# Group norm of each image moved from VectorE to ScalarE and GpSimd in the loop over chunks of a two-layer state-space model

## The chip, the cores and the metric

The kernel runs on one core of one Trainium2 chip. Time is device time in microseconds (us), as the median of several executions. The engines of the core are TensorE (PE in the profile), VectorE (DVE), ScalarE (ACT), GpSimd (POOL) and SyncE (SP), which issues most DMAs. Each engine has its own stream of instructions, worked off in order; they wait for each other by semaphores.

## The reference, cut to what matters

An image tensor x of shape (4, 128, 64, 64), called (b, t, n, f), goes through four residual layers. Layers 0 and 1 are the ones that the change is about: a group norm over (t, n) and pairs of features, then a Mamba block along t for each of the 4 x 64 sequences.

```python
def _gn(v, G=32, eps=1e-5):          # v: (B, H, W, C)
    g = v.reshape(B_, H_, W_, G, C_ // G)
    m = jnp.mean(g, axis=(1, 2, 4), keepdims=True)
    s = jnp.var(g, axis=(1, 2, 4), keepdims=True)
    return ((g - m) / jnp.sqrt(s + eps)).reshape(v.shape)

x = x + _L0_conv_ref(_gn(x), ...)    # Mamba, 64 features in, 128 inner, 16 states
x = x + _L1_conv_ref(_gn(x), ...)    # the same with other weights
x = x + _L2_conv_ref(_gn(x), ...)    # top 25 pixels of 16 blocks, two large products
x = x + _L3_conv_ref(_gn(x))         # attention at three scales
```

Mamba is h = exp(dt * A) * h + dt * u * B, y = sum over states of h * C, for 16 states of each of 128 channels.

## The kernel before, in words

X stays in SBUF all the time: 128 partitions are t, and one image is 4096 columns (n, f). Layers 0 and 1 are one loop, `mamba_layers`: an image is cut into 8 chunks of 8 sequences, which makes 32 chunks for each layer and 64 in all (`TOTAL`). A chunk is worked in 16 units, one for each state: a decay on ScalarE (line 742), a drive on VectorE (772) or, for the five states of `POOL_UNITS`, on GpSimd (820), a scan on VectorE (786), the product with C on GpSimd (826), and the sum on TensorE (660). Beside unit s of chunk c stands step s of the preparation of chunk c + 1 (`*_prep`: u, B and C, dt, z), and the gate (791) and the addition to X (795) of chunk c - 1. Every engine's order within a unit is written out in `act_both`, `dve_unit`, `pool_unit` and `pe_unit`. Four buffers of state and of decay let the engines run a few units apart.

The norm is a class, `ImageNorm`. Job j belongs to image j mod 4; jobs 0 to 3 are the input of layer 0, 4 to 7 that of layer 1, and 8 and 9 already images 0 and 1 of layer 2. A job is 32 `bn_stats` on VectorE (206), short VectorE steps on 128 x 32 numbers (217 to 242) with two sums over partitions on TensorE and a Ln and Exp on ScalarE between, and the turning of scale and bias into one column for each feature (251, 265, 276). `NORM_AT` says in which chunk a job begins; its steps are spread over four chunks by `STEP_AT`, and all 32 `bn_stats` stand together at the end of unit 15 of every eighth chunk (and of chunks 0 and 4). Job 0 is done in `prepare`, a block of its own in front of the loop, beside the turning of the weights; the block ends for all engines together. There SyncE issues the load of all four images at once, and ScalarE the 18 small loads of weights.

Layer 2 begins with a group norm on VectorE again (`GroupNorm`, lines 93 to 135, called in `top_blocks`); before, it does images 2 and 3 only (`first` = 2). TensorE's part of it stands behind the scores and fourteen turned pairs.

## Time and profile before

| | us |
|---|---|
| median of 3 executions | 6269.2 (6269.18 to 6271.9) |
| the profiled execution, its own time | 6272.24 |
| span of the profile | 6270.4 |
| first drive of chunk 0 (line 772) starts | 85.09 |
| first drive of chunk 63, the last, starts | 3817.41 |
| granted TensorE clock, mean | 0.932 |

The profile is of one execution. Its times count from the start of the span. "Busy" is the time in which an engine executes something; "idle before" is the engine's gap in front of an instruction, with what released it. The loop over chunks takes 3.73 ms of the 6.27 ms; layer 2 and layer 3 (attention) follow. A chunk is best measured from its first drive to that of the next.

### The profile page before, as it was taken

To read this page: it belongs to the slowest core of one execution; us is meant where nothing else is said; L and a number is where in the kernel's file an instruction comes from. 1 tells how busy PE (TensorE), PEld (TensorE's weight loads), DVE (VectorE), ACT (ScalarE), POOL (GpSimd) and SP (SyncE) were. 2 spreads that over 40 slices of the span, in tenths; PEclk is the share of its full clock that TensorE was granted. 3 is DMA by queue.
4 is the path that set the end of the run, shared out by engine and by line. 5 is a ranking of instruction groups with operands and counts; after the bars stand their busy time and mean duration, and the time that the engine had idled before them with its cause. 6 is when DMAs were issued, how large, how long until landed. Compare 5 with 4: busy or idle time off the path is not lost. (4 is left out here: it accounts for less than half of the span.)

```text
span 6270.4 us, 72602 instructions
## 1 busy us (share of the span) xinstructions
PE 5117.5 (82%) x22494; PEld 2648.8 (42%) x22494; DVE 5045.7 (80%) x7034; ACT 3286.3 (52%) x3657; POOL 4771.9 (76%) x2169
## 2 busy tenths in 40 slices
...
GB/s 154 190 188 184 183 192 205 190 185 205 190 187 205 186 188 205 189 188 206 186 193 206 195 193 155 124 404 74 72 93 164 189 166 190 181 173 189 189 188 209
DMA packets 1424093, 1152.34 MB, mean 184 GB/s; under 512 B 1216728, under 2 KB 1226096, under 8 KB 1415792
## 3 DMA queue, kind: packets, MB, share of 16 engines
...
q8 instruction: 105, 1.72, 0.1%
...
HBM read 814.23 MB, written 21.09 MB: 133 GB/s over the span
## 5 line engine op out<-in xcount | busy, mean ns | idle before, releaser
L826 POOL TENSOR_TENSOR mamba_state<-mamba_state,mamba_c_row 128x1024 f32<-128x1024 f32 x1024 | 2408.9, 2364 | 221.4 <-DVE mamba_state L786 212.0
L660 PE MATMUL mamba_y_ps<-mamba_state,ident 128*128 128x512 f32 x4096 | 2003.9, 616 | 28.5 <-POOL mamba_state L826 28.2
L1721 POOL TENSOR_TENSOR l3s_el<-l3s_s_sb,l3s_eh 128x1024 f16<-128x1024 f32 (+2 forms) x584 | 1169.5, 2013 | 1119.3 <-ACT l3s_s_sb L1706 1113.2
L786 DVE TENSOR_TENSOR_SCAN mamba_state<-mamba_decay,mamba_b_ps 128x1024 f32<-128x1024 f32 x704 | 1607.7, 2284 | 64.3 <-DVE mamba_b_ps L772 2.4
L660 PEld LDWEIGHTS mamba_y_ps<-mamba_state,ident 128*128 128x128 f32 x4096 | 789.5, 196 | 853.4 <-issue 689.2
L1729 DVE TENSOR_SCALAR_CACHE_REDUCE l3s_s_sb<-l3s_s_ps 128x512 f32<-128x512 f32 (+1 forms) x1096 | 753.2, 688 | 479.4 <-PE l3s_s_ps L1665 455.0
L1678 PE MATMUL l3s_o_ps<-l3s_vt,l3s_et 128*128 128x257 f16 x4368 | 879.7, 279 | 189.9 <-DMA l3s_et<-l3s_el 124.8
L742 ACT ACTIVATE mamba_decay<-mamba_dt,mamba_A 128x1016 f32<-128x1016 f32 x704 | 785.9, 1133 | 292.3 <-POOL mamba_dt L807 190.7
L1705 ACT ACTIVATE l3s_eh<-l3s_s_sb,l3s_shift 128x1024 f16<-128x1024 f32 (+2 forms) x584 | 634.6, 1087 | 535.8 <-DMA l3s_et<-l3s_el 423.7
L648 PE MATMUL mamba_b_ps<-mamba_bc,mamba_pick 128*128 128x512 f32 x1408 | 580.7, 495 | 400.2 <-DVE mamba_state L786 392.8
L772 DVE TENSOR_TENSOR mamba_b_ps<-mamba_dtu,mamba_b_ps 128x1024 f32<-128x1024 f32 x704 | 850.4, 1208 | 32.8 <-PE mamba_b_ps L648 31.7
L1680 PE MATMUL l3s_o_ps<-l3s_vt,l3s_et 128*128 128x129 f16 x4368 | 788.5, 224 | 0.0
L820 POOL TENSOR_TENSOR mamba_b_row<-mamba_b_row,mamba_dtu 128x1024 f32<-128x1024 f32 x320 | 755.2, 2360 | 0.1
L786 DVE TENSOR_TENSOR_SCAN mamba_state<-mamba_b_ps,mamba_b_row 128x1024 f32<-128x1024 f32 x320 | 729.3, 2279 | 3.5 <-POOL mamba_b_row L820 1.6
L1706 ACT ACTIVATE l3s_s_sb<-l3s_s_sb,l3s_shift 128x1024 f32<-128x1024 f32 (+2 forms) x584 | 630.0, 1079 | 0.0
L1678 PEld LDWEIGHTS l3s_o_ps<-l3s_vt,l3s_et 128*128 128x128 f16 x4368 | 434.9, 100 | 438.2 <-issue 214.9
L648 PEld LDWEIGHTS mamba_b_ps<-mamba_bc,mamba_pick 128*128 128x128 f32 x1408 | 234.3, 200 | 863.0 <-DVE mamba_state L786 567.6
L1663 PE MATMUL l3s_s_ps<-l3s_xh 128*128 128x512 f16 (+1 forms) x1096 | 428.0, 390 | 94.3 <-DVE l3s_xl L1642 71.4
L1680 PEld LDWEIGHTS l3s_o_ps<-l3s_vt,l3s_et 128*128 128x128 f16 x4368 | 435.2, 100 | 109.9 <-issue 5.7
L1664 PE MATMUL l3s_s_ps<-l3s_xl,l3s_xh 128*128 128x512 f16 (+1 forms) x1096 | 427.2, 390 | 0.0
L1665 PE MATMUL l3s_s_ps<-l3s_xh,l3s_xl 128*128 128x512 f16 (+1 forms) x1096 | 426.2, 389 | 0.0
L742 ACT ACTIVATE mamba_b_ps<-mamba_dt,mamba_A 128x1016 f32<-128x1016 f32 x320 | 351.5, 1098 | 0.0
...
## 6 DMA issues: line engine op xcount, KB each, us to landing
mamba_c_row<-mamba_c_rows SPq DMA_DIRECT2D x1024, 512.0 KB, 3.7
mamba_b_row<-mamba_c_rows SPq DMA_DIRECT2D x320, 512.0 KB, 4.8
...
l_ring_a<-in_L_conv_W SPq DMA_DIRECT2D x14, 704.0 KB, 12.7
l2b_ring_b<-in_L_conv_W SPq DMA_DIRECT2D x13, 704.0 KB, 12.7
...
```

The source lines that it names most:

```text
L648: last = nc.tensor.matmul(b_ps[s % PAIRS][:, half(h)], C["pick"][:, DVE_UNITS.index(s) * P:(DVE_UNITS.index(s) + 1) * P], bc[:, par, half( ...
L660: last = nc.tensor.matmul(y_ps[:, half(h)], C["ident"][:, :], state[:, s % STATES, half(h)], start=False, stop=(s == S - 1))
L742: nc.scalar.activation(seq(to), seq(dt[:, par, :]), ACT.Exp, scale=weights(c)["A"][:, s:s + 1]).then_inc(s_decay, 1)
L772: nc.vector.tensor_tensor(b_ps[s % PAIRS][:, :], dtu[:, par, :], b_ps[s % PAIRS][:, :], ALU.mult).then_inc(s_drive, 1)
L786: nc.vector.tensor_tensor_scan(state[:, s % STATES, :], by, add, 0.0, ALU.mult, ALU.add).then_inc(s_scan, 1)
L820: nc.gpsimd.tensor_tensor(row, row, dtu[:, par, :], ALU.mult).then_inc(s_bdrive, 1)
L826: nc.gpsimd.tensor_tensor(state[:, s % STATES, :], state[:, s % STATES, :], c_row[:, s % C_ROWS, :], ALU.mult).then_inc(s_hc, 1)
L1678: high = lambda stop: nc.tensor.matmul(o_ps[par][:, 0:2 * P + 1], et[:, 0, slot, j, :], vt[:, mt, 0:2 * P + 1], start=(mt == 0), stop=stop)
L1680: lows = lambda: nc.tensor.matmul(o_ps[par][:, P:2 * P + 1], et[:, 1, slot, j, :], vt[:, mt, P:2 * P + 1], start=False, stop=False)
L1705: nc.scalar.activation(eh[:, part, off:off + EXPW], src, ACT.Exp, bias=shift[:, par:par + 1]).then_inc(s_eh, 1)
L1721: nc.gpsimd.tensor_tensor(el[:, part, off:off + EXPW], s_sb[:, par, j * EXPW:(j + 1) * EXPW], eh[:, part, off:off + EXPW], ALU.subtract).t ...
L1729: nc.vector.tensor_scalar(s_sb[:, par, kb * W:(kb + 1) * W], s_ps[(par * NB + kb) % SLOTS][:, 0:W], 0.0, None, ALU.add, ALU.max, accum_out ...
```

## The change

- In the loop VectorE has nothing of the norm any more. For layer 1 (jobs 4 to 7) the statistics of an image are taken by ScalarE in 64 passes over 128 x 128 numbers: 32 that add up the values of a pair of features, and 32 that add up the squares of the distance from the partition's own mean (`scalar_stats`). They are spread over eight chunks, 8 for each chunk (`stat_at`, `STAT_UNITS`).
- The short steps of a job are ten on ScalarE (`scalar`) and six on GpSimd (`gpsimd`), spread over five chunks by `ACT_AT` and `POOL_AT`.
- The statistics of images 1 to 3 for layer 0 stay `bn_stats` on VectorE, but all stand in the preparation of chunk 0, in front of steps 4, 10 and 13 (`SECOND_STATS`), each with six short steps behind them.
- `ImageNorm` no longer does jobs 8 and 9: the norm in front of layer 2 takes all four images.
- SyncE loads image 0 first, and the other three when all weights have landed.
- In `prepare`, the chain of job 0 goes over ScalarE and GpSimd, and the second layer's weights are turned behind its first two sums.

```diff
+    def vector_stats(self, dve, j):
+
+        nc, mine, m2 = self.nc, self.mine[:, self.groups(j)], self.m2[:, self.groups(j)]
+        for g in range(G):
+            nc.vector.bn_stats(out=self.stats[:, g * 6:(g + 1) * 6],
+                               in_=self.Xv[:, j, :, 2 * g:2 * g + 2]).then_inc(self.s_stats, 1)
+        dve.wait_ge(self.s_stats, G * (j + 1))
+        st = self.stats.rearrange("p (g k) -> p g k", k=6)
+        nc.vector.tensor_tensor(self.dev[:, :], st[:, :, 1], st[:, :, 4], ALU.subtract)
+        nc.vector.tensor_tensor(m2, st[:, :, 2], st[:, :, 5], ALU.add)
+        nc.vector.tensor_tensor(mine, st[:, :, 1], st[:, :, 4], ALU.add).then_inc(self.s_join, 1)
+        dve.wait_ge(self.s_join, 3 * j + 1)
+        nc.vector.tensor_scalar(mine, mine, 0.5, None, ALU.mult)
+        nc.vector.tensor_tensor(self.square[:, :], self.dev[:, :], self.dev[:, :], ALU.mult).then_inc(self.s_join, 1)
+        dve.wait_ge(self.s_join, 3 * j + 2)
+        nc.vector.scalar_tensor_tensor(m2, self.square[:, :], N / 2.0, m2, ALU.mult, ALU.add).then_inc(self.s_join, 1)
+
+    def scalar_stats(self, act, j, k):
+
+        nc, later = self.nc, j - B
+        image = self.Xv[:, j % B, :, :]
+        group = lambda g: image[:, :, 2 * g:2 * g + 2]
+        over = self.over.rearrange("p (n e) -> p n e", e=2)
+        g = k % G
+        if k < G:
+            wait(act, self.s_first, G * later + g)
+            if g == 0:
+                wait(act, self.s_second, G * later)
+            nc.scalar.activation(over, group(g), ACT.Identity, accum_out=self.sums[:, g:g + 1]).then_inc(self.s_first, 1)
+            return
+        if g == 0:
+            act.wait_ge(self.s_first, G * (later + 1))
+            nc.scalar.activation(self.mine[:, self.groups(j)], self.sums[:, :], ACT.Identity,
+                                 scale=0.5 / N).then_inc(self.s_centre, 1)
+            nc.scalar.activation(self.minus[:, :], self.sums[:, :], ACT.Identity, scale=-0.5 / N).then_inc(self.s_centre, 1)
+            act.wait_ge(self.s_centre, 2 * (later + 1))
+        wait(act, self.s_second, G * later + g)
+        at = j % B * G + g
+        nc.scalar.activation(over, group(g), ACT.Square, bias=self.minus[:, g:g + 1],
+                             accum_out=self.m2[:, at:at + 1]).then_inc(self.s_second, 1)
...
+    def scalar(self, act, ps, j, i):
...
+            act.wait_ge(self.s_sum, 3 * j + 1)
+            op = nc.scalar.activation(self.mean[:, :], ps[:, 0:G], ACT.Identity, scale=1.0 / P)
...
+        if i in (7, 8):
+            act.wait_ge(self.s_pool, pool_done + 6)
+            src = (self.scale_g, self.bias_g)[i - 7][0:1, self.groups(j)]
+            for copy in range(2):
+                dst = self.rows[0:1, i - 7, copy * F:(copy + 1) * F].rearrange("p (g e) -> p g e", e=2)
+                op = nc.scalar.activation(dst, src.unsqueeze(2).to_broadcast([1, G, 2]), ACT.Identity,
+                                          scale=(1.0, -1.0)[i - 7])
...
+    def gpsimd(self, pool, j, i):
+        nc, act_done, pool_done = self.nc, ACT_STEPS * j, POOL_STEPS * j
+        square, root, m2 = self.square[:, :], self.root[:, :], self.m2[:, self.groups(j)]
+        scale, bias = self.scale_g[:, self.groups(j)], self.bias_g[:, self.groups(j)]
+        if i == 0:
+            pool.wait_ge(self.s_act, act_done + 1)
+            op = nc.gpsimd.tensor_tensor(self.dev[:, :], self.mine[:, self.groups(j)], self.mean[:, :], ALU.subtract)
+        if i == 1:
+            pool.wait_ge(self.s_act, act_done + 3)
+            if j >= B:
+                pool.wait_ge(self.s_second, G * (j - B + 1))
+            op = nc.gpsimd.tensor_tensor(m2, m2, square, ALU.add)
...
+ACT_STEPS, POOL_STEPS = 10, 6
...
             @block.sync
             def _(sp):
                 for b in range(B):
+                    if b == 1:
+                        for i in range(2):
+                            sp.wait_ge(s_load[i], len(WEIGHTS) * 16)
                     sp.dma_start(X[:, b * PIX:(b + 1) * PIX], ins["x"][b].rearrange("t n f -> t (n f)")).then_inc(s_x[b], 16)
 
             @block.gpsimd
...
+                norm.constants(pool)
+                for i in range(POOL_STEPS):
+                    norm.gpsimd(pool, 0, i)
...
+                act.wait_ge(norm.s_const, 2)
+                for i in range(ACT_STEPS):
+                    norm.scalar(act, sum_ps[(0, 0, 0, 1, 1, 1, 1, 0, 0, 0)[i]], 0, i)
...
+                scale_taps(0)
                 dve.wait_ge(s_x[0], 16)
-                for g in range(G):
-                    norm.stat(0, g)
-                norm.step(dve, 0, 0)
+                norm.vector_stats(dve, 0)
                 copy_turned(0)
-                norm.step(dve, 0, 1)
-                norm.step(dve, 0, 2)
-                norm.read(dve, sum_ps[0], 0, 0)
-                for i in range(3, 6):
-                    norm.step(dve, 0, i)
+                scale_taps(1)
...
+                turn(0)
                 pe.wait_ge(s_one, 1)
                 norm.sum(pe, sum_ps[0], 0, 0)
-                pe.wait_ge(s_wdt[0], 1)
-                nc.tensor.matmul(f_ps[0][:, 0:D], wx[0][0:R, :], wdt_t[0][:, :], start=True, stop=True).then_inc(s_fused[0], 1)
+                fuse(0)
                 norm.sum(pe, sum_ps[1], 0, 1)
-                pe.wait_ge(s_wdt[1], 1)
-                nc.tensor.matmul(f_ps[1][:, 0:D], wx[1][0:R, :], wdt_t[1][:, :], start=True, stop=True).then_inc(s_fused[1], 1)
+                turn(1)
                 norm.sum(pe, sum_ps[0], 0, 2)
+                fuse(1)
...
+NORM_AT = [None] + [5 * (j - 1) for j in range(1, B)] + [PER_IMAGE * (j - B + 2) + 1 for j in range(B, 2 * B)]
+NORM_JOB = {first + phase: (j, phase) for j, first in enumerate(NORM_AT) if first is not None for phase in range(5)}
+SECOND_STATS = {4: 1, 10: 2, 13: 3}
+SUM_AT, SUMS = 14, {0: 0, 1: 1, 3: 2}
+ACT_AT = ({}, {1: 0, 6: 1, 7: 2}, {1: 3, 2: 4, 6: 5, 13: 6}, {6: 7, 7: 8}, {1: 9})
+POOL_AT = ({}, {3: 0, 10: 1}, {8: 2, 10: 3, 15: 4}, {1: 5}, {})
+STAT_UNITS = (2, 6, 7, 10, 13, 14, 15, 16)
+
+
+def stat_at(c, s):
+
+    if s == 0:
+        c, s = c - 1, S
+    if s not in STAT_UNITS or c <= PER_IMAGE:
+        return None
+    j, slot = divmod((c - PER_IMAGE - 1) * len(STAT_UNITS) + STAT_UNITS.index(s), 2 * G)
+    return (j + B, slot) if j < B else None
...
-                    wait(pe, norm.s_read, norm_reads_before(n - 1))
...
+            stat = stat_at(c, s)
+            if stat:
+                if stat[1] == 0:
+                    act.wait_ge(s_add, PER_IMAGE * (stat[0] - B + 1))
+                norm.scalar_stats(act, *stat)
+
+        def pool_norm(pool, c, s):
+            j, phase = NORM_JOB.get(c, (None, None))
+            if j is not None and s in POOL_AT[phase]:
+                norm.gpsimd(pool, j, POOL_AT[phase][s])
 
...
         def act_both(act, c, par, s, prep):
             act_unit(act, c, par, s)
+            act_norm(act, c, s)
             if prep:
                 act_prep(act, c + 1, 1 - par, s)
-            act_norm(act, c, s)
...
-            dve_norm(dve, c, s)
...
-            dve_stats(dve, c, s)
...
+            pool_norm(pool, c, s)
...
                 for k in range(S):
-                    if k == 4:
-                        dve.wait_ge(s_x[1], 16)
-                        for g in range(G):
-                            norm.stat(1, g)
+                    if k in SECOND_STATS:
+                        dve.wait_ge(s_x[SECOND_STATS[k]], 16)
+                        norm.vector_stats(dve, SECOND_STATS[k])
                     dve_prep(dve, 0, 0, k)
...
-                           offset[:, :, :, :].rearrange("p a r k -> p (a r k)")[:, 0:B * G * 6], temps, pick_ps[0], pick_ps[1], 2)
+                           offset[:, :, :, :].rearrange("p a r k -> p (a r k)")[:, 0:B * G * 6], temps, pick_ps[0], pick_ps[1])
```

VectorE before, at the border of chunks 16 and 17, where job 5 begins. `mamba_state` is the scan, `X<-X` the addition of a finished chunk.

```order
L795 TENSOR_TENSOR X<-X,mamba_prep_ps 128x512
L786 SCALAR_TENSOR_TENSOR mamba_state<-mamba_decay,mamba_b_ps 128x1024
L206 BN_STATS mamba_norm_stats<-X 128x6 x32
L772 TENSOR_TENSOR mamba_b_ps<-mamba_dtu,mamba_b_ps 128x1024
L786 SCALAR_TENSOR_TENSOR mamba_state<-mamba_decay,mamba_b_ps 128x1024
L772 TENSOR_TENSOR mamba_b_ps<-mamba_dtu,mamba_b_ps 128x1024
L217 TENSOR_TENSOR mamba_norm_dev<-mamba_norm_stats 128x32
L218 TENSOR_TENSOR mamba_norm_spread<-mamba_norm_stats 128x32
L219 TENSOR_TENSOR mamba_norm_pair_sum<-mamba_norm_stats 128x32
```

The same place in the changed kernel:

```order
L840 TENSOR_TENSOR X<-X,mamba_prep_ps 128x512
L831 SCALAR_TENSOR_TENSOR mamba_state<-mamba_decay,mamba_b_ps 128x1024
L817 TENSOR_TENSOR mamba_b_ps<-mamba_dtu,mamba_b_ps 128x1024
L831 SCALAR_TENSOR_TENSOR mamba_state<-mamba_decay,mamba_b_ps 128x1024
L817 TENSOR_TENSOR mamba_b_ps<-mamba_dtu,mamba_b_ps 128x1024
L831 SCALAR_TENSOR_TENSOR mamba_state<-mamba_decay,mamba_b_ps 128x1024
L836 TENSOR_TENSOR mamba_yz<-mamba_sz,mamba_y_ps 128x1024
```

All the `norm` rows of this place are gone from VectorE, and the scans and drives follow each other.

GpSimd before, from the drive of the last of its states in a chunk (`mamba_b_row` is a drive, `mamba_state` a product, `mamba_ln_e` and `mamba_dt` preparation):

```order
L820 TENSOR_TENSOR mamba_b_row<-mamba_b_row,mamba_dtu 128x1024
L826 TENSOR_TENSOR mamba_state<-mamba_state,mamba_c_row 128x1024 x3
L803 TENSOR_TENSOR mamba_ln_e<-mamba_ln_e,mamba_gu 128x1024
L826 TENSOR_TENSOR mamba_state<-mamba_state,mamba_c_row 128x1024
L807 TENSOR_TENSOR mamba_dt<-mamba_ln_e,mamba_dt 128x1024
L826 TENSOR_TENSOR mamba_state<-mamba_state,mamba_c_row 128x1024
L813 TENSOR_TENSOR mamba_dtu<-mamba_dt,mamba_u 128x1024
```

The same place in the changed kernel, in a chunk with the third phase of a job:

```order
L871 TENSOR_TENSOR mamba_state<-mamba_state,mamba_c_row 128x1024 x2
L865 TENSOR_TENSOR mamba_b_row<-mamba_b_row,mamba_dtu 128x1024
L323 TENSOR_TENSOR mamba_norm_square<-mamba_norm_root 128x32
L871 TENSOR_TENSOR mamba_state<-mamba_state,mamba_c_row 128x1024 x2
L326 TENSOR_TENSOR mamba_norm_square<-mamba_norm_square,mamba_norm_var 128x32
L871 TENSOR_TENSOR mamba_state<-mamba_state,mamba_c_row 128x1024
L848 TENSOR_TENSOR mamba_ln_e<-mamba_ln_e,mamba_gu 128x1024
L871 TENSOR_TENSOR mamba_state<-mamba_state,mamba_c_row 128x1024
L852 TENSOR_TENSOR mamba_dt<-mamba_ln_e,mamba_dt 128x1024
L871 TENSOR_TENSOR mamba_state<-mamba_state,mamba_c_row 128x1024
```

Two of the six short steps of a job stand here between products of 128 x 1024.

ScalarE before, units 6 to 9 of a chunk. `mamba_decay` and `mamba_b_ps` are decays, the rest preparation.

```order
L742 ACTIVATE mamba_b_ps<-mamba_dt,mamba_A 128x8x127
L742 ACTIVATE mamba_decay<-mamba_dt,mamba_A 128x8x127
L738 ACTIVATE mamba_b_ps<-mamba_zero 128x8
L742 ACTIVATE mamba_b_ps<-mamba_dt,mamba_A 128x8x127
L706 ACTIVATE mamba_dt<-mamba_prep_ps,mamba_b_dt 128x1024
L708 ACTIVATE mamba_prep_ps<-mamba_prep_ps,mamba_b_dt 128x1024
L710 ACTIVATE mamba_prep_ps<-mamba_prep_ps 128x1024
L742 ACTIVATE mamba_decay<-mamba_dt,mamba_A 128x8x127
```

The same place in the changed kernel, in one of the chunks 9 to 41; the rows with `norm_sums` are the new passes over X:

```order
L787 ACTIVATE mamba_b_ps<-mamba_dt,mamba_A 128x8x127
L243 ACTIVATE mamba_norm_shared,mamba_norm_sums<-X 128x128
L787 ACTIVATE mamba_decay<-mamba_dt,mamba_A 128x8x127
L243 ACTIVATE mamba_norm_shared,mamba_norm_sums<-X 128x128
L783 ACTIVATE mamba_b_ps<-mamba_zero 128x8
L787 ACTIVATE mamba_b_ps<-mamba_dt,mamba_A 128x8x127
L751 ACTIVATE mamba_dt<-mamba_prep_ps,mamba_b_dt 128x1024
L753 ACTIVATE mamba_prep_ps<-mamba_prep_ps,mamba_b_dt 128x1024
L755 ACTIVATE mamba_prep_ps<-mamba_prep_ps 128x1024
L787 ACTIVATE mamba_decay<-mamba_dt,mamba_A 128x8x127
```

The two passes of units 6 and 7 stand behind the decays of these units, in front of the step that waits for dt.

## Rows read from the trace of the kernel before

**Rows 1.** Rows of the page, part 1: busy us (share of the span) xinstructions.

```profile
PE 5117.5 (82%) x22494; PEld 2648.8 (42%) x22494; DVE 5045.7 (80%) x7034; ACT 3286.3 (52%) x3657; POOL 4771.9 (76%) x2169
```

**Rows 2.** Busy time by window: bounds, length; PE, PEld, DVE, ACT, POOL busy (x); clock, DMA.

```profile
824.89:1052.57 227.68, 198.55 (x558) 89.65 (x556) 219.43 (x133) 126.23 (x140) 223.07 (x96) 0.97 0.58 201
...
3185.08:3469.59 284.51, 246.93 (x695) 112.00 (x693) 274.15 (x166) 158.43 (x176) 278.93 (x120) 0.97 0.58 201
...
3648.09:3817.41 169.32, 146.81 (x414) 66.22 (x412) 164.37 (x100) 94.65 (x105) 167.28 (x72) 0.98 0.57 200
...
85.09:3817.41 3732.32, 3148.02 (x8733) 1421.46 (x8731) 3618.36 (x2531) 1990.70 (x2224) 3515.71 (x1511) 0.96 0.56 192
```

**Rows 3.** Groups by line, 0 to 4200 us: busy, mean ns | idle before, releaser.

```profile
L826 POOL TENSOR_TENSOR mamba_state<-mamba_state,mamba_c_row 128x1024 f32<-128x1024 f32 x1024 | 2408.9, 2364 | 221.4 <-DVE mamba_state L786 212.0
...
L786 DVE TENSOR_TENSOR_SCAN mamba_state<-mamba_decay,mamba_b_ps 128x1024 f32<-128x1024 f32 x704 | 1607.7, 2284 | 64.3 <-DVE mamba_b_ps L772 2.4
```

**Rows 4.** VectorE in order of time: start, us, line, operation [idle before].

```profile
1003.69 1.20 DVE L791 TENSOR_TENSOR mamba_yz<-mamba_sz,mamba_y_ps 128x1024 f32<-128x1024 f32 x1
...
1030.29 1.20 DVE L760 SCALAR_TENSOR_TENSOR mamba_gu<-mamba_gu,mamba_prep_ps 128x1024 f32<-128x1024 f32 x1
...
1059.67 1.20 DVE L791 TENSOR_TENSOR mamba_yz<-mamba_sz,mamba_y_ps 128x1024 f32<-128x1024 f32 x1
...
1108.68 6.25 DVE L206 BATCH_NORM_STATS2 mamba_norm_stats<-X 128x6 f32<-128x128 f32 x32
```

**Rows 5.** Groups by line, 0 to 4200 us: the norm on VectorE.

```profile
L206 DVE BATCH_NORM_STATS2 mamba_norm_stats<-X 128x6 f32<-128x128 f32 x320 | 62.6, 278 | 0.3 <-PEq L319 0.3
...
L242 DVE SCALAR_TENSOR_TENSOR bias_g<-mamba_norm_mean,scale_g 128x32 f32<-128x32 f32 x10 | 15.1, 1508 | 0.0
...
L240 DVE TENSOR_TENSOR scale_g<-mamba_norm_root,mamba_norm_square 128x32 f32<-128x32 f32 x10 | 13.1, 1308 | 0.0
```

**Rows 6.** GpSimd groups by form: one operation at two sizes.

```profile
L1721 POOL TENSOR_TENSOR l3s_el<-l3s_s_sb,l3s_eh 128x1024 f16<-128x1024 f32 x512 | 1090.2, 2141 | 509.0 <-ACT l3s_s_sb L1706 502.9
...
L1721 POOL TENSOR_TENSOR l3s_el<-l3s_s_sb,l3s_eh 128x256 f16<-128x256 f32 x8 | 5.4, 670 | 477.7 <-ACT l3s_s_sb L1706 477.7
```

**Rows 7.** ScalarE in order of time, the same chunk as group 4.

```profile
1021.14 0.18 ACT L738 ACTIVATE mamba_b_ps<-mamba_zero 128x8 f32<-128x8 f32 x1 [1.93 <-DVE mamba_state L786]
...
1027.51 1.02 ACT L715 ACTIVATE mamba_gu<-mamba_prep_ps 128x1024 f32<-128x1024 f32 x1
```

**Rows 8.** DMA throughput, 0 to 100 us in 40 slices of 2.5 us.

```profile
GB/s 85 344 426 427 426 428 433 434 377 76 4 0 0 3 0 0 0 0 105 0 105 0 0 0 0 0 20 72 265 315 397 243 0 0 7 0 36 346 88 162
```

**Rows 9.** All engines in order of time, the first 46 us.

```profile
6.21 12.96 ACTq L346 DMA_DIRECT2D start_cw<-in_L_conv_conv_w  x1
...
24.80 1.28 ACT L354 ACT_TABLE_LOAD   x1 [24.80 <-issue]
...
28.50 6.26 DVE L206 BATCH_NORM_STATS2 mamba_norm_stats<-X 128x6 f32<-128x128 f32 x32
...
40.50 0.23 ACT L282 ACTIVATE mamba_norm_root<-mamba_norm_var 128x32 f32<-128x32 f32 x1 [13.04 <-DVE mamba_norm_var L274]
...
44.91 0.16 DVE L276 COPY mamba_norm_c<-start_sum_ps 128x2 f32<-128x2 f32 x1 [1.16 <-PE start_sum_ps L265]
```

**Rows 10.** All engines in order of time, preparation of chunk 0.

```profile
76.44 1.22 DVE L760 SCALAR_TENSOR_TENSOR mamba_gu<-mamba_gu,mamba_prep_ps 128x1024 f32<-128x1024 f32 x1 [8.69 <-ACT mamba_gu L715]
...
77.82 2.35 POOL L803 TENSOR_TENSOR mamba_ln_e<-mamba_ln_e,mamba_gu 128x1024 f32<-128x1024 f32 x1 [32.22 <-DVE mamba_gu L760]
...
83.10 1.23 DVE L764 TENSOR_TENSOR mamba_sz<-mamba_prep_ps,mamba_gz 128x1024 f32<-128x1024 f32 x1 [5.44 <-ACT mamba_gz L724]
...
85.09 1.23 DVE L772 TENSOR_TENSOR mamba_b_ps<-mamba_dtu,mamba_b_ps 128x1024 f32<-128x1024 f32 x1 [0.76 <-POOL mamba_dtu L813]
```

**Rows 11.** VectorE in order of time, head of layer 2.

```profile
3887.13 13.09 DVE L102 BATCH_NORM_STATS2 l2a_offset<-X  x64 [4.89 <-PEq L70]
...
3931.13 0.22 DVE L119 SCALAR_TENSOR_TENSOR l2a_shared<-l2a_shared,l2a_pick_ps 128x64 f32<-128x64 f32 x1 [29.72 <-PE l2a_pick_ps L139]
```

More of the change, by code:

```diff
@@ L195, in __init__ @@
+        self.s_second = sem("norm_second_pass")
         self.s_sum = sem("norm_sum_over_partitions")
[L196 to L207 removed]
@@ L209, in step @@
[L209 to L219 removed]
+        self.s_act = sem("norm_scalar_step")
@@ new lines, in sum @@
+    def sum(self, pe, ps, j, k):
+        nc = self.nc
+        if k < 2:
+            if k == 1:
+                pe.wait_ge(self.s_pool, POOL_STEPS * j + 2)
+            elif j < B:
+                pe.wait_ge(self.s_join, 3 * j + 3)
+            else:
+                pe.wait_ge(self.s_centre, 2 * (j - B + 1))
+            src = (self.mine, self.m2)[k]
+            last = nc.tensor.matmul(ps[:, 0:G], self.C["one"][:, :], src[:, self.groups(j)], start=True, stop=True)
+        if k == 2:
+            pe.wait_ge(self.s_act, ACT_STEPS * j + 9)
+            for i in range(2):
+                last = nc.tensor.matmul(ps[:, i:i + 1], self.rows[0:1, i, :], self.C["one"][0:1, 0:1], start=True, stop=True)
+        last.then_inc(self.s_sum, 1)
@@ L254, in sum @@
-    def sum(self, pe, ps, j, k):
-        wait(pe, self.s_read, self.reads(j) + k)
-        if k == 0:
-            pe.wait_ge(self.s_step, NORM_STEPS * j + 1)
-            last = self.nc.tensor.matmul(ps[:, 0:G], self.C["one"][:, :], self.pair_sum[:, :], start=True, stop=True)
-        if k == 1:
-            pe.wait_ge(self.s_step, NORM_STEPS * j + 6)
-            last = self.nc.tensor.matmul(ps[:, 0:G], self.C["one"][:, :], self.spread[:, :], start=True, stop=True)
-        if k == 2:
-            pe.wait_ge(self.s_rows, 8 * (j + 1))
-            for i in range(2):
-                last = self.nc.tensor.matmul(ps[:, i:i + 1], self.rows[0:1, i, :, :].rearrange("p c f -> p (c f)"),
-                                             self.C["one"][0:1, 0:1], start=True, stop=True)
-        last.then_inc(self.s_sum, 1)
@@ L411, in _ @@
                     nc.vector.tensor_copy(C["pick"][:, i * P:(i + 1) * P], pick[:, unit * P:(unit + 1) * P])
-                for i in range(6, NORM_STEPS):
-                    norm.step(dve, 0, i)
-                norm.row(dve, 0, 0)
-                norm.row(dve, 0, 1)
-                norm.read(dve, sum_ps[0], 0, 2)
             @block.tensor
```

177 lines of the change are left out of this document (62 added, 115 removed).

## The prediction

> **What bounds the kernel now.** I read the counts of the page first, then busy time by window, then VectorE, GpSimd and ScalarE in order of time. The page [rows 1] gives VectorE 80% and GpSimd 76% of the span, an average over stages that says little. The windows tell it [rows 2]: each is cut at the first drive of a chunk. Three of them, of 4, 5 and 3 chunks, hold nothing of the norm: 227.68 + 284.51 + 169.32 = 681.5 us for 12 chunks, 56.8 us each, with GpSimd busy 669.3 us (98%) and VectorE 658.0 us (97%). The whole loop up to the last chunk takes 3732.32 us for 63 chunks, 59.2 us each. There VectorE is busy 57.4 us for each chunk, and GpSimd 55.8 us, which is no more than in the windows without a norm. So two engines are almost equally full: GpSimd with 24 operations of 128 x 1024 for each chunk, VectorE with scans and drives [rows 3]. A job of the norm lies on VectorE and stops both: GpSimd's idle time in the loop is nearly all a wait for a scan [rows 3].
>
> The best chunk takes 55.98 us, from gate to gate [rows 4]: the 288 GpSimd operations of the three windows are busy 669.3 us, 2.32 each, and 24 of them are 55.8 us. The 0.8 us that an average chunk without a norm takes above that comes in chunks in which TensorE's clock was granted at the lower level for a while; the windows stand at 0.97 and 0.98 of full speed [rows 2]. I keep these stalls in the forecast.
>
> **The loop.** Removed from VectorE are the 32 `bn_stats` of jobs 2 to 9, 6.25 us at a stretch [rows 4], and some 22 short steps of jobs 1 to 9. The short steps are dear: two of them take 1.5 and 1.3 us for 32 columns [rows 5], while a `bn_stats` over 128 columns takes 0.28. By VectorE's busy time the norm is 57.4 - 54.8 = 2.6 us for each chunk, 164 us in 63. Not all of it comes back, since behind VectorE stands GpSimd at 98%. What comes back is the difference of the periods: 63 x 56.8 = 3578.4, so 3732.3 - 3578.4 = **153.9 us less**.
>
> **GpSimd's new steps.** Jobs 1 to 7 have six each, 42 operations on 128 x 32, on an engine that has no room. The trace has the same operation at 1024 and at 256 columns, 2.141 and 0.670 us [rows 6]: 1.9 ns for each column and 0.18 us fixed, an estimate of 0.25 us at 32. From below stands the fixed part, 0.18 us, from above the 0.67 us of 256 columns: 7.6 to 28 us in all. I take 42 x 0.25 = **10.5 us more**. Their waits: each waits for a ScalarE or GpSimd step placed two or more units earlier, and behind a waiting one stand GpSimd's products, for which TensorE and, over the four state buffers, the scans wait. ScalarE runs ahead of GpSimd, so I put these waits at nothing; if a step waited 1 us each time, it would cost 42 us.
>
> The operations of VectorE in rows 5 with two operands in SBUF take five times as long as the `bn_stats`, which has one. The Trainium skill (SBUF — State Buffer, Who interferes with whom) says that a VectorE instruction with two SBUF inputs and a GpSimd instruction that reads SBUF exclude each other, and that the second one blocks fully; the trace agrees. By that rule GpSimd's new steps too could be held by VectorE, but after the change each VectorE instruction of the loop has at most one operand in SBUF, beside one in PSUM, so the sum would stay as it is; by equal sharing the steps would cost up to the upper bound.
>
> **ScalarE's new work.** 256 passes over 128 x 128, eight for each chunk from 9 to 41, and seven times ten short steps. ScalarE is busy 126.2 us in four chunks [rows 2], 31.6 us of 56.9. A pass with the reading of its sum I put at 0.5 us, above the 0.23 us of 128 x 32 [rows 9] and well under the 1.02 us of 128 x 1024 [rows 7]: 4 us for each chunk, up to 8 us by the upper bound. They cost nothing as long as no decay and no preparation step gets late. The tight place is units 6 and 7: two passes and, in a job, two short steps, 1.5 us, stand in front of a wait of 1.93 us [rows 7]; and behind it the step at line 715 ends at 1028.5 while VectorE takes its result at 1030.29 [rows 4], without a gap in front, 1.8 us later. So 3.7 us of cover against 1.5 us; at the upper bound 2.5 us, still covered. The passes at 13 to 16 stand where ScalarE is ahead of the scans.
>
> **The start.** SyncE's four loads keep the DMA engines at about 430 GB/s until 22.5 us [rows 8], ScalarE's queue is held for 12.96 us at its 11th load, and its table load comes at 24.80 us [rows 9]. With image 0 alone the transfer is over after about 7.5 us (the first three slices of rows 8 hold its 2.1 MB). The held load is then free at about 8.5 us, seven more at 0.6 us each, as the first ten took without a jam (6.21 us), end at 12.7 us, table and first Exp at 14.2 us, and the `bn_stats` of job 0 start at 14.4 instead of 28.50 us [rows 9]: 14.1 us earlier. From there to the last step of the block it was 16.6 us (45.07 - 28.50) [rows 9]. Now: `bn_stats` and joining 7.2 us, the chain over ScalarE, GpSimd and TensorE with some twenty steps of 0.25 to 0.35 us (a short ScalarE step is 0.23 [rows 9]) about 6.5 us, then the last fused product and the copies on VectorE behind it 3 us: 16.7. **14 us less**; between 8 us (a longer chain, ring still jammed) and 17 us.
>
> In chunk 0's preparation VectorE idles 8.69 us before line 760 and 5.44 us before line 764 [rows 10]. The second image's statistics there (6.3 + 1.1 us) fit into the first gap; the third's (7.4 us and more, since GpSimd works beside it from 77.82 us [rows 10]) overrun the second by 2.6 us, with 0.76 us of slack behind it: **2.6 us more**, at most 6. The images have landed by then: issued at 14.5 us, at 430 GB/s until about 30 us.
>
> **Layer 2.** `GroupNorm` takes four images instead of two: 13.09 us more of `bn_stats`. VectorE waits 29.72 us for TensorE right behind it [rows 11], so that is hidden; 64 more columns in ten short steps and a reciprocal behind the wait are **1.2 us more**. At most 3.
>
> **Sum.** -153.9 + 10.5 - 14 + 2.6 + 1.2 = -153.6. The profiled execution's own time is 6272.24 us, 3.0 above the median of the three runs: 6272.2 - 153.6 = 6118.6, and 6115.6 as a median. I predict **6116 us**, a ratio of 0.9755.
>
> **Rivals.** (1) The stalls of the low TensorE clock go with the norm, and the loop settles at 55.98 us a chunk: 63 x 0.82 = 52 us less, 6064. For it: single chunks reach that [rows 4]. Against: the windows without a norm have the stalls too, and average 56.8 [rows 2]. (2) GpSimd is now the only bound, and its steps cost the upper bound and wait: 28 + 21 (0.5 us each), in place of 10.5: 6155. (3) The start gives only 4 us of its 14, because ScalarE's 18 issues or the longer chain over three engines set its end: 6126. (4) The other side: ScalarE's passes are slow, since they read pairs 256 bytes apart, and hold up the preparation. It decides once two passes and two steps at units 6 and 7 exceed 3.7 us; to undo the whole gain, each of 33 chunks must lose 4.6 us, so a pass must take about 4 us. The same reading on VectorE runs at full pace (0.28 us, rows 5). Half of that would leave 6190; all of it 6280. (5) The first `tensor_tensor` on GpSimd now comes in the chain of job 0. In the trace it starts 0.16 us after its release, with 32 us of idle time before it [rows 10]; what may load in that time needs cover, of which about 14 us are left. If none covered it, it would be some 6 us, 6122. The Trainium skill (GPSIMD Engine Reference, Instruction dispatch) says that the first call of newly loaded code costs about 6 us that no row shows; by that rule 6122, if it counts from the call; the trace does not bear that out.
>
> **Chances.** Forecast 58% (own range 6095 to 6140), rival 1 12%, rival 2 14%, rival 3 7%, rival 5 4%, rival 4 5%, of which 2.5% slower than before. Eight in ten lie in 6072 to 6165: all of the forecast and of rivals 3 and 5, most of rival 2, and the nearer part of 1. 0.2% (13 us) is about what a measurement of this kernel can tell from none: faster by more 0.965, within 0.01, slower 0.025.
>
> **What would show it.** Chunks of 56 to 58 us from first drive to first drive, with GpSimd over 97% busy and VectorE at 96%; GpSimd's small steps at 0.2 to 0.3 us and without waits; ScalarE's passes under 0.6 us, and no new wait of VectorE at lines 760 and 764 of the old numbering; `bn_stats` of job 0 at about 14.4 us and the first drive of chunk 0 at about 74 us; the head of layer 2 within 2 us of before. It is wrong if VectorE or GpSimd shows gaps behind ScalarE, if chunks take over 57.5 us, or if the start moves by less than 8 us.

## The result and the profile after

The changed kernel takes 6103.5 us (median of four runs, 6098.0 to 6112.2); the kernel before, beside it on the same chip, 6269.7. The ratio is 0.9736, with a 95% interval of [0.9719, 0.9752]. The prediction said 6116 us and 0.9755. The profiled execution is the slowest of the four, 6112.24 us, where the prediction's sum gave 6118.6: 160.0 us were gained in place of 153.6. The medians lie further apart, 12 us, because the profiled execution is 8.7 us above its median here, and 3.0 us before.

The page, part 1, and busy time by window from the first drive of chunk 0 to that of the last chunk, and for three chunks that follow one another (columns as in [rows 2]):

```profile
PE 5081.1 (83%) x22486; PEld 2628.5 (43%) x22486; DVE 4908.9 (80%) x6708; ACT 3384.9 (55%) x4253; POOL 4779.0 (78%) x2219
```

```profile
73.72:3656.23 3582.51, 3115.66 (x8726) 1404.66 (x8726) 3453.06 (x2079) 2087.51 (x2809) 3518.44 (x1552) 0.97 0.57 201
...
1664.64:1720.62 55.98, 48.44 (x138) 21.84 (x138) 54.73 (x35) 34.56 (x56) 55.93 (x26) 0.98 0.56 204
1720.62:1778.76 58.14, 50.60 (x144) 23.23 (x142) 54.94 (x34) 35.75 (x54) 55.93 (x25) 0.96 0.58 199
1778.76:1835.30 56.54, 49.49 (x138) 22.29 (x138) 54.83 (x35) 34.19 (x51) 55.79 (x24) 0.97 0.57 201
```

Against [rows 2] the loop went from 3732.32 to 3582.51 us, 149.8 less; the start moved the first drive from 85.09 to 73.72, 11.4 less; from the last chunk's first drive to the end it is 2454.2 us, 1.2 more. VectorE lost 165 us of work, ScalarE got 97 us more, GpSimd has as much as before. The sequence 55.98, 58.14, 56.54 comes back in a part of the loop (chunks 22 to 33); elsewhere it is irregular.

The two groups of [rows 3] and ScalarE's passes:

```profile
L871 POOL TENSOR_TENSOR mamba_state<-mamba_state,mamba_c_row 128x1024 f32<-128x1024 f32 x1024 | 2410.7, 2371 | 70.6 <-DVE mamba_state L831 62.5
...
L831 DVE TENSOR_TENSOR_SCAN mamba_state<-mamba_decay,mamba_b_ps 128x1024 f32<-128x1024 f32 x704 | 1609.1, 2286 | 78.8 <-ACT mamba_b_ps L787 1.5
```

```profile
L243 ACT ACTIVATE mamba_norm_shared<-X x128: 292/299/321, 587.6 to 2168.3; 128x128 f32<-128x128 f32 x128
L243 ACT ACTIVATION_READ_ACCUMULATOR mamba_norm_shared<-X x128: 185/187/209, 587.8 to 2168.5; 128x1 f32 x128
```

(In the last two rows: ns, shortest, median and longest.) GpSimd's wait for scans fell from 212 to 62.5 us. What VectorE waits for in the loop (us in total, times, longest):

```profile
DVE mamba_b_ps L817 <- PE mamba_b_ps L693: 30.7, 40, 1.1
DVE mamba_yz L836 <- PE mamba_y_ps L705: 17.2, 18, 1.9
DVE mamba_state L831 <- ACT mamba_b_ps L787: 1.5, 3, 0.5
```

It waits for TensorE, hardly for ScalarE. The start, which answers to [rows 9], and the preparation of chunk 0, which answers to [rows 10]:

```profile
6.12 0.99 ACTq L399 DMA_DIRECT2D start_cw<-in_L_conv_conv_w  x1
...
10.99 1.28 ACT L407 ACT_TABLE_LOAD   x1 [10.99 <-issue]
...
12.62 6.27 DVE L219 BATCH_NORM_STATS2 mamba_norm_shared<-X 128x6 f32<-128x128 f32 x32
21.05 0.25 POOL L315 TENSOR_TENSOR mamba_norm_minus<-mamba_norm_mine,mamba_norm_mean 128x32 f32<-128x32 f32 x1 [13.62 <-ACT mamba_norm_mean L278]
...
27.24 0.17 ACT L306 ACTIVATE mamba_norm_c<-start_sum_ps 128x2 f32<-128x2 f32 x1 [1.10 <-PE start_sum_ps L270]
```

```profile
61.03 1.22 DVE L805 SCALAR_TENSOR_TENSOR mamba_gu<-mamba_gu,mamba_prep_ps 128x1024 f32<-128x1024 f32 x1 [1.30 <-ACT mamba_gu L760]
62.17 6.27 DVE L219 BATCH_NORM_STATS2 mamba_norm_shared<-X 128x6 f32<-128x128 f32 x32
...
69.72 2.34 POOL L865 TENSOR_TENSOR mamba_b_row<-mamba_b_row,mamba_dtu 128x1024 f32<-128x1024 f32 x1
69.76 2.37 DVE L225 TENSOR_TENSOR mamba_norm_mine<-mamba_norm_shared 128x32 f32<-128x32 f32 x1
...
72.58 1.22 DVE L809 TENSOR_TENSOR mamba_sz<-mamba_prep_ps,mamba_gz 128x1024 f32<-128x1024 f32 x1
73.72 1.22 DVE L817 TENSOR_TENSOR mamba_b_ps<-mamba_dtu,mamba_b_ps 128x1024 f32<-128x1024 f32 x1
```

The held load takes 0.99 us in place of 12.96. The step at line 225 has 32 columns and lasts 2.37 us, as long as the GpSimd operation that started 0.04 us before it. The head of layer 2 answers to [rows 11]: the wait shrank from 29.72 to 18.41 us, and covers the longer statistics.

```profile
3723.38 24.81 DVE L102 BATCH_NORM_STATS2 l2a_offset<-X  x128 [5.06 <-PEq L70]
...
3768.26 0.29 DVE L119 SCALAR_TENSOR_TENSOR l2a_shared<-l2a_shared,l2a_pick_ps 128x128 f32<-128x128 f32 x1 [18.41 <-PE l2a_pick_ps L139]
```

### The profile page after: what moved, and what is told of

Same layout as the page of the kernel before. It is cut to its first block and busy times, and to the rows that moved or that the text cites. A ratio compares the mean times of both kernels' runs of the same rounds, so it can differ in the third digit from the quotient of the medians.

```text
span 6110.4 us, 72884 instructions
## 1 busy us (share of the span) xinstructions
PE 5081.1 (83%) x22486; PEld 2628.5 (43%) x22486; DVE 4908.9 (80%) x6708; ACT 3384.9 (55%) x4253; POOL 4779.0 (78%) x2219
## 5 line engine op out<-in xcount | busy, mean ns | idle before, releaser
L871 POOL TENSOR_TENSOR mamba_state<-mamba_state,mamba_c_row 128x1024 f32<-128x1024 f32 x1024 | 2410.7, 2371 | 70.6 <-DVE mamba_state L831 62.5
L817 DVE TENSOR_TENSOR mamba_b_ps<-mamba_dtu,mamba_b_ps 128x1024 f32<-128x1024 f32 x704 | 850.8, 1209 | 30.8 <-PE mamba_b_ps L693 30.7
## 6 DMA issues: line engine op xcount, KB each, us to landing
l_ring_a<-in_L_conv_W SPq DMA_DIRECT2D x14, 704.0 KB, 12.7
l2b_ring_b<-in_L_conv_W SPq DMA_DIRECT2D x13, 704.0 KB, 12.7
```

The lines of the kernel that those rows point to most:

```text
L817: nc.vector.tensor_tensor(b_ps[s % PAIRS][:, :], dtu[:, par, :], b_ps[s % PAIRS][:, :], ALU.mult).then_inc(s_drive, 1)
L871: nc.gpsimd.tensor_tensor(state[:, s % STATES, :], state[:, s % STATES, :], c_row[:, s % C_ROWS, :], ALU.mult).then_inc(s_hc, 1)
```

## Experiments

Times are medians of five runs or more, each with its ratio to the kernel before and the 95% interval of that. The runs were made in three sets of four, on three chips, where the kernel before had 6267.5, 6265.5 and 6267.0 us; the changed kernel was repeated in the first set alone, and "more" and "less" below are against that repeat, with an uncertainty of several us. The best chunk is the shortest from first drive to first drive; its length, which many chunks share, is called the floor.

**The changed kernel again.**

> The changed kernel once more, unedited, so that the others of this chip can be set against it. All theories: 6098 to 6112 us, ratio to the kernel before 0.9736 within 0.001; first drive of chunk 0 at about 73.7 us; best chunks 55.98 us from first drive to first drive.

6102.4 us, ratio 0.9741 [0.9727, 0.9754]; first drive at 73.68, loop 3575.46 us. The two profiles of one program differ by 7 us in the loop (3582.51 and 3575.46), though their floors are 55.98 and 55.97 us (chunk 0, which has no gate before it, is left out). So a few us in the loop are not read from single profiles below.

**Which engine is the floor of a chunk?** First VectorE is given less to do:

```
-            nc.vector.tensor_tensor(X[:, columns(c)], X[:, columns(c)], prep_ps[:, 0:COLS],
+            nc.vector.tensor_tensor(X[:, some], X[:, some], prep_ps[:, 0:64],      # some: the first 64
```

> The update of X in each chunk is narrowed to 64 of its 512 columns (seven eighths of the update is left out), which takes about 0.45 us from VectorE in each of 64 chunks and nothing from GpSimd. Theory V (VectorE's own chain is the floor of a chunk, GpSimd has some 0.25 us to spare): the best chunk falls from 55.98 to about 55.7 us, where GpSimd's 24 operations stand, and the time by 15 to 30 us. Theory G (GpSimd at 24 operations is the floor, as the prediction had it): best chunk 55.98 us as before, time within 6 us of the changed kernel.

6086.3 us, ratio 0.9713 [0.97, 0.9726], 16 less than the changed kernel; the best chunk is 55.60 us instead of 55.97. The update and the scan behind it, in the changed kernel and in this one:

```profile
1717.82 0.68 DVE L840 TENSOR_TENSOR X<-X,mamba_prep_ps 128x512 f32<-128x512 f32 x1
1718.42 2.28 DVE L831 TENSOR_TENSOR_SCAN mamba_state<-mamba_decay,mamba_b_ps 128x1024 f32<-128x1024 f32 x1
...
3118.19 0.21 DVE L841 TENSOR_TENSOR X<-X,mamba_prep_ps 128x64 f32<-128x64 f32 x1
3118.41 2.29 DVE L831 TENSOR_TENSOR_SCAN mamba_state<-mamba_decay,mamba_b_ps 128x1024 f32<-128x1024 f32 x1
```

The record of the update shrank by 0.47 us. From its start to that of the scan, though, it went from 0.59 to 0.22 us (medians of the loop), 0.37 less, and the floor fell by the same 0.37. So all that VectorE's chain lost came off the floor. GpSimd did not keep single chunks from reaching 55.60 us; where its own bound lies, this run does not show. Then GpSimd is given more:

```
+            if s in EXTRA_AT:      # (5, 12)
...
+                nc.gpsimd.tensor_tensor(extra[:, :], extra[:, :], extra[:, :], ALU.mult).then_inc(s_extra, 1)
```

> Two more GpSimd operations of 128 x 32 in each of 64 chunks, after units 5 and 12, each waiting for nothing but the one before: 0.25 us each, 32 us in all. Theory G: the whole is paid, about +30 us, best chunk 56.5 us. Theory V: the first 0.25 us of each chunk are free and the rest is paid: best chunk 56.2 us, +10 to +18 us.

6107.4 us, ratio 0.9752 [0.9739, 0.9766], 5 more, 3.2 of them in the loop, and the best chunk stays at 55.97. GpSimd in order of time, around one extra operation, then the loop of this kernel and that of the repeat:

```profile
1060.72 2.37 POOL L875 TENSOR_TENSOR mamba_state<-mamba_state,mamba_c_row 128x1024 f32<-128x1024 f32 x1
1063.03 0.26 POOL L958 TENSOR_TENSOR mamba_extra<-mamba_extra 128x32 f32<-128x32 f32 x1
1063.22 2.38 POOL L875 TENSOR_TENSOR mamba_state<-mamba_state,mamba_c_row 128x1024 f32<-128x1024 f32 x1
1065.54 2.37 POOL L869 TENSOR_TENSOR mamba_b_row<-mamba_b_row,mamba_dtu 128x1024 f32<-128x1024 f32 x1
```

```profile
75.39:3654.01 3578.62, 3110.85 (x8725) 1395.48 (x8726) 3451.85 (x2079) 2086.23 (x2809) 3538.03 (x1678) 0.97 0.58 201
...
73.68:3649.14 3575.46, 3111.78 (x8726) 1404.58 (x8726) 3452.14 (x2078) 2087.57 (x2809) 3516.85 (x1552) 0.97 0.58 201
```

From start to start a long operation takes 2.31 to 2.32 us here, less than its recorded 2.37, and the extra one takes 0.19, not 0.26. Records that follow each other overlap, so the mean of the records overstates an operation; the busy time of a window counts the overlap once. By that busy time GpSimd needs 3516.85 / 63 = 55.8 us in a chunk, some 55.7 without the norm's short steps. VectorE's own chain is 55.97: 54.73 us of work and 11 gaps of 0.11 us on average, each between a drive and the scan that reads it. So GpSimd has some 0.3 us to spare in the best chunk and 0.9 us in an average one (58.6 us idle in 63). The extra steps made it busy for 21.2 us more, and 3.2 of these reached the loop.

Theory G falls: neither its +30 us nor its best chunk of 56.5 came. VectorE is the floor, as theory V has it, but V's figures (+10 to +18 us, a best chunk of 56.2) were missed too, since it took 0.25 us for a step and the room of the best chunk for that of every chunk.

**Are short steps dear on VectorE?**

```
-            pool_norm(pool, c, s)       # in pool_unit
...
             dve_scan(dve, c, par, s)
+            pool_norm(dve, c, s)        # its tensor_tensor on nc.vector
```

> GpSimd's six short steps of jobs 1 to 7 (42 in all) run on VectorE, behind the scan of the same unit; job 0 keeps them on GpSimd. Theory of dear steps (a VectorE step with two operands in SBUF waits while GpSimd works, 1.3 to 1.5 us as in the kernel before): the steps last 1.3 us or more, 42 x 1.3 = 55 us, so +45 to +60 us. Theory of plain length: 0.15 to 0.3 us each, +6 to +12 us.

6108.0 us, ratio 0.9746 [0.9733, 0.976], 5.7 more: near plain length. The 42 steps last 0.16 to 0.50 us. VectorE and GpSimd in order of time at two of the steps, and in the kernel before at one that was dear:

```profile
243.35 2.39 POOL L872 TENSOR_TENSOR mamba_state<-mamba_state,mamba_c_row 128x1024 f32<-128x1024 f32 x1
...
246.42 0.16 DVE L330 TENSOR_TENSOR scale_g<-mamba_norm_root,mamba_norm_square 128x32 f32<-128x32 f32 x1
...
246.58 2.36 POOL L872 TENSOR_TENSOR mamba_state<-mamba_state,mamba_c_row 128x1024 f32<-128x1024 f32 x1 [0.84 <-DVE mamba_state L832]
...
2551.34 0.40 DVE L324 TENSOR_TENSOR mamba_norm_square<-mamba_norm_root 128x32 f32<-128x32 f32 x1
2551.65 2.37 POOL L866 TENSOR_TENSOR mamba_b_row<-mamba_b_row,mamba_dtu 128x1024 f32<-128x1024 f32 x1
```

```profile
1263.38 2.36 POOL L820 TENSOR_TENSOR mamba_b_row<-mamba_b_row,mamba_dtu 128x1024 f32<-128x1024 f32 x1
1264.36 1.43 DVE L236 TENSOR_TENSOR mamba_norm_square<-mamba_norm_square,mamba_norm_var 128x32 f32<-128x32 f32 x1
1265.69 4.72 POOL L826 TENSOR_TENSOR mamba_state<-mamba_state,mamba_c_row 128x1024 f32<-128x1024 f32 x2
```

The dear step ends at 1265.79, 0.05 us after the GpSimd operation that was running (1265.74). The cheap one at 246.42 finds GpSimd waiting for the scan. So the length of such a step is what is left of GpSimd's running operation: in the loop of the kernel before, all 92 steps that met an operation with more than 0.15 us left ended 0.05 to 0.07 us behind it. Behind a scan GpSimd is often between two. The Trainium skill (SBUF — State Buffer, Who interferes with whom) has a VectorE instruction with two SBUF inputs contend with a GpSimd instruction that reads SBUF, for ports that only one of them can hold. These rows agree, and show that the price depends on the place.

The same move was tried in the kernel before:

```
-            if s in STEP_AT[phase]:                     # ahead of dve_scan
-                norm.step(dve, j, STEP_AT[phase][s])
...
             dve_scan(dve, c, par, s)
+            dve_steps(dve, c, s)                        # the same steps
```

> The kernel before, with VectorE's eleven steps of each norm job moved from ahead of the scan of their unit to right behind it; nothing else is changed, the statistics stay on VectorE. Theory that a VectorE step with two operands in SBUF lasts until GpSimd's running operation has ended, and that behind a scan GpSimd is between two operations: the single steps shrink from 0.6 to 1.65 us to 0.2 to 0.5 us, some 5 us for each of nine jobs, and the time is 30 to 50 us below the kernel before. Theory that such a step is dear wherever it stands: within 10 us of the kernel before.

6258.9 us, ratio 0.9991 [0.9982, 1.0]: 7 less, by its time the second theory's outcome. The groups by line of the steps, of this kernel, up to the last chunk:

```profile
L219 DVE TENSOR_TENSOR mamba_norm_pair_sum<-mamba_norm_stats 128x32 f32<-128x32 f32 x9 | 21.4, 2380 | 0.0
L240 DVE TENSOR_TENSOR scale_g<-mamba_norm_root,mamba_norm_square 128x32 f32<-128x32 f32 x9 | 11.3, 1256 | 0.0
...
L242 DVE SCALAR_TENSOR_TENSOR bias_g<-mamba_norm_mean,scale_g 128x32 f32<-128x32 f32 x9 | 1.5, 166 | 0.0
```

The steps show the first theory's mechanism, with places that it had wrong. The one at line 242 fell from 1654 to 166 ns, but the third of three in a row went from 203 to 2380, since it meets the GpSimd operation that the scan released, and lines 240 and 236 stayed above 1.1 us. The 13 groups sum to 7.1 us for each job instead of 10.5, 31 us in all, and the loop gave 13 of these back. Where the other 18 went is open.

**What does the new work in the loop cost?** All of it is left out:

```
-NORM_JOB = {first + phase: (j, phase) for j, first in enumerate(NORM_AT) if first is not None for phase in range(5)}
+NORM_JOB = {}        # and stat_at returns None
```

> Jobs 1 to 7 are left out of the loop: no pass and no short step on ScalarE, no short step on GpSimd, no sum on TensorE; every image takes the scale and shift of image 0. Theory V with free ScalarE work: within 6 us of the changed kernel. If GpSimd's 42 steps cost what was predicted: 10 us less; if ScalarE's passes hold up the preparation: more than 15 us less.

6098.8 us, 3.6 less, ratio 0.973 [0.9717, 0.9744]; the loop takes 3574.53 us against 3575.46 with the norm, with 100 us less on ScalarE (1987.23 against 2087.57). That is the first theory's outcome, but the intervals of the two kernels overlap, and two profiles of one program differ by 7 us, so this run alone doesn't exclude the 10 us of the second. The extra GpSimd steps do: 128 of them cost 3 to 5 us, which makes 1 to 2 us for 42. And ScalarE's passes done twice:

```
+            nc.scalar.activation(over, group(g), ACT.Identity, accum_out=self.sums[:, g:g + 1]).then_inc(self.s_twice, 1)
+            act.wait_ge(self.s_twice, 2 * G * later + g + 1)
```

> Each of ScalarE's 256 passes over the image is done twice (some 0.5 us more, eight times in each chunk from 9 to 41, 130 us of ScalarE in all). If the passes have cover everywhere (the forecast's 3.7 us against 1.5 us at units 6 and 7): within 8 us of the changed kernel. If the cover is just about used up: 20 to 60 us more, with VectorE waiting at its steps of units 10 and 13 or at the scans for a decay.

6102.0 us, ratio 0.9741 [0.9728, 0.9754], the same as the changed kernel. ScalarE is busy 2202.9 us in the loop (2086.4 before the edit), and VectorE's waits for it stay at some 2 us. The passes have cover to spare.

**The kernel before with the statistics of four images in layer 2.**

```
-NORM_JOBS = 2 * B + 2
+NORM_JOBS = 2 * B
```

> The kernel before, with jobs 8 and 9 left out of the loop and the statistics of all four images taken in the head of layer 2: that part of the change alone. Two of nine jobs, some 18 us of VectorE each in the trace, 150 us for nine: 30 to 38 us less, minus 1 us in layer 2. If the head of layer 2 is not covered: 13 us of that come back, 18 to 24 us less.

6243.3 us, ratio 0.9963 [0.9951, 0.9975]: 24 less, and 26 in the loop. It lies at the edge of the second theory, but not by its mechanism: in this kernel too VectorE's wait for TensorE behind the statistics shrank, from 29.72 to 18.04 us, and covers them. Two jobs are worth 13 us each, below the mean of 17 for nine (150 / 9); jobs 8 and 9 had two sums each, not three, and no rows to write, which may be why.

**The start.** All images are loaded at once again:

```
-                    if b == 1:
-                        for i in range(2):
-                            sp.wait_ge(s_load[i], len(WEIGHTS) * 16)
```

> SyncE issues the loads of all four images at once, as in the kernel before; the rest is the changed kernel. If the start gained by the order of the loads: ScalarE's queue is held again for about 13 us, the statistics of job 0 start at about 26 to 28 us in place of 12.6, the first drive of chunk 0 at 85 to 88 us, and the time is 11 to 15 us above the changed kernel. If it gained by the shorter work on VectorE alone: within 4 us of it.

6114.1 us, ratio 0.9758 [0.9744, 0.9771], 12 more; statistics of job 0 at 26.86 us, first drive at 86.95, 13.3 us later. The order of the loads is the whole gain of the start. The new chain of job 0 gives none: from the statistics to the end of the block it is 17.3 us, and was 16.9. Then the statistics are placed anew:

```
-SECOND_STATS = {4: 1, 10: 2, 13: 3}
+SECOND_STATS = {4: (1, 2), 10: (3,)}
```

> In the preparation of chunk 0 the statistics of images 1 and 2 both stand before VectorE's step of unit 4 (a gap of some 14 us), those of image 3 before the step of unit 10, none before unit 13, where they overran by about 4 us. First drive of chunk 0 at about 70 us in place of 73.7, the time 3 to 4 us less. Rival (the steps beside GpSimd were already hidden): first drive within 1 us of 73.7.

6099.1 us, ratio 0.9733 [0.972, 0.9746], 3.3 less; first drive at 71.05, and VectorE again waits ahead of it:

```profile
69.09 1.23 DVE L809 TENSOR_TENSOR mamba_sz<-mamba_prep_ps,mamba_gz 128x1024 f32<-128x1024 f32 x1 [5.44 <-ACT mamba_gz L769]
71.05 1.23 DVE L817 TENSOR_TENSOR mamba_b_ps<-mamba_dtu,mamba_b_ps 128x1024 f32<-128x1024 f32 x1 [0.74 <-POOL mamba_dtu L858]
```

In this profile everything ahead was later than in the repeat (line 805 at 62.43 us, and 60.99 there), as in some other runs (see the last section). From line 805 to the first drive it is 8.6 us in place of 12.7: the whole overrun of 4.1 us is gone, and the first drives, set side by side, hide a part of that.

**The chunks above the floor.** In the changed kernel TensorE's clock falls to half (0.50 granted, the level of 1.2 GHz) for 3.4 us, rarely for 6.8, at two places of a chunk. TensorE in order of time ahead of one dip, then windows ahead of it and in two of the dips:

```profile
1750.66 3.44 PE L705 MATMUL mamba_y_ps<-mamba_state,ident 128*128 128x512 f32 x7
1756.49 2.08 PE L682 MATMUL mamba_prep_ps<-mamba_xt,mamba_w_z 64*128 64x512 f32 x4 [2.40 <-DVE mamba_gu L805]
```

```profile
1718.90:1722.20 3.30, 3.30 (x7) 1.43 (x6) 3.17 (x3) 0.00 (x0) 3.23 (x2) 0.50 0.56 187
1756.50:1759.80 3.30, 3.30 (x7) 1.60 (x8) 2.18 (x2) 1.12 (x2) 3.30 (x3) 0.50 0.39 158
1750.00:1756.40 6.40, 4.09 (x10) 1.43 (x8) 6.27 (x5) 6.01 (x9) 6.40 (x3) 1.00 0.48 166
```

TensorE idles 2.40 us, waiting for VectorE, and the clock falls right behind it. At the border of two chunks (the dip at 1718.9) it idles 0.85 and 0.81 us before. In the profile of the unedited repeat there are 44 dips at 34 to 38 us of a chunk and 15 at its end. The gap alone doesn't make a dip: it is 2.1 to 2.4 us too in the 18 other chunks behind chunk 0, where the clock stays up, as it does behind the gaps of some 1 us at 21, 28 and 44 us of a chunk. The gap of 2.4 us is filled with work that adds nothing:

```
             if k == 10:
+                if n > 0:
+                    for h in range(2):
+                        nc.tensor.matmul(y_ps[:, half(h)], still[:, :], weights(n)["w_u"][64:128, 0:HALF],
+                                         start=False, stop=False)
                 wait(pe, s_lost, n + 1)
```

> TensorE fills the gap in which it waits for VectorE before the z product: two matmuls of a zero 64 x 128 weight tile against 64 x 512 columns are added into y (adding nothing), once in each chunk but the first. Theory that the idle time calls the lower clock: the dips at about 36 us into a chunk (3.4 us each, in the trace of the changed kernel right behind a gap of 2.4 us) become rare, the average chunk goes from 56.8 towards 56.0 us, 20 to 50 us less. Theory that the dips come whatever TensorE does there: as many dips, time within 6 us of the changed kernel, or up to 15 us more where the filler itself comes in the way.

6080.0 us, 22 less, ratio 0.9704 [0.969, 0.9717]. No dip at 34 to 38 us is left. At the end of chunks there are 25, ten more than in the repeat, so some seem to have moved there. The average chunk is 56.39 us. So the two other gaps were filled too, one matmul each, with the edit to the statistics beside it:

```
+            if s == 0 and c > 0:    # ahead of pe_rows, and once more behind it with half(1)
+                nc.tensor.matmul(y_ps[:, half(0)], still[:, :], weights(c)["w_u"][64:128, 0:HALF],
+                                 start=False, stop=False)
```

> Both edits that helped (the filler ahead of the z product, the statistics of images 1 and 2 in the first gap), and two more filler matmuls at the start of each chunk, one ahead of the rows of unit 0 and one ahead of the sum that follows: there TensorE idles 1.15 and 0.79 us in the traces, and 25 dips of the clock remained right behind it. Theory that TensorE's gaps call the dips: these 25 go too, the average chunk falls from 56.4 to about 56.0 us, and the time to 6040 to 6060 us (22 + 3 + some 25 us below the changed kernel). Rival (the filler delays the rows that VectorE waits for, or the dips come elsewhere): 6075 us or more.

**6054.7 us**, ratio 0.9664 [0.965, 0.9677], 48 below the changed kernel. The loop, and VectorE's drives:

```profile
71.42:3600.83 3529.41, 3274.79 (x9229) 1431.61 (x9227) 3446.13 (x2077) 2085.63 (x2810) 3516.90 (x1553) 1.00 0.59 204
```

```profile
L824 DVE TENSOR_TENSOR mamba_b_ps<-mamba_dtu,mamba_b_ps 128x1024 f32<-128x1024 f32 x694 | 837.1, 1206 | 0.7 <-POOL mamba_dtu L865 0.7
```

The clock stands at 1.00, with a single dip left, in chunk 0; 63 chunks take 56.02 us each, and VectorE no longer waits for TensorE at its drives. The loop is at VectorE's floor. GpSimd is idle for 12.5 us of it, so it would bound the loop next, some 0.3 us a chunk below.

## Why the prediction came out as it did

- **The loop without the norm, -153.9.** The size is right. With the new work at 1 us, the two profiles of the changed kernel give -150.8 and -157.9. The period comes from windows without a norm and holds whatever bounds them. The reason given, that GpSimd keeps back the rest, does not hold: the chunks stand on VectorE's chain and on the dips of TensorE's clock.
- **GpSimd's new steps, +10.5.** This is the term that was mis-sized: by the extra steps it is 1 to 2 us, and the loop without the norm is 0.9 us shorter. Their length was right (0.26 us recorded, 0.21 from start to start). The step that failed is "on an engine that has no room". By the prediction's own windows GpSimd is idle for 12.2 of 681.5 us, 1.0 us in each chunk. The 55.98 us of [rows 4] is VectorE's chain; the prediction set it beside GpSimd's 24 x 2.32 = 55.8 and took the near match for a bound. That the steps wait for nothing was right (idle time 0.0).
- **ScalarE's passes, nothing.** Right: a pass is 0.30 us (sums) or 0.39 (squares) and 0.19 for reading the sum, and twice as many cost nothing.
- **The start, -14 and +2.6.** The statistics of job 0 began at 12.62, not 14.4, since the held load was free at 7.1 us, not 8.5, and the seven behind it took 0.55 us each; the block ended 15.4 us earlier. The third image's statistics overran by 4.1 us, not 2.6: two of the joining steps waited for GpSimd, 1.24 and 2.37 us, the very rule that the prediction cites for the loop. Nor does its working give the 2.6, for 7.4 us less the gap of 5.44 and the slack of 0.76 is 1.2. That the sum is right, -11.4 against -11.4, is luck: the two errors cancel.
- **Layer 2, +1.2.** The statistics are covered, as said. The steps behind the wait take 4.9 us in place of 4.1, so 0.8 more (from line 119 to the first step behind the norm). That the whole time from the last chunk's first drive on grew by just 1.2 us is chance: it is 2454.2 us in this profile and 2448.7 in that of the repeat.
- **Rivals.** The code load of rival 5 does not show: GpSimd's first `tensor_tensor` takes 0.25 us, and ScalarE has its result 0.3 us after its start. The 13.62 us of idle time ahead of it may have covered a load, so the rule of the Trainium skill (GPSIMD Engine Reference, Instruction dispatch) is not refuted, but it set nothing here. Rivals 2, 3 and 4 are excluded by the extra steps, the start and the doubled passes. Rival 1 did not happen, for the reason given (57 dips in the loop without a norm), and its price, 52 us in 63 chunks, is what the fillers later gave: 46 in the loop.
